# Attention and experts in one pipelined kernel: another order of the small steps in the second half of each batch

## The chip, the cores and the metric

The kernel runs on one core of a Trainium2 chip. The metric is the device time of one execution in microseconds (us). All engines of the core take part: TensorE (PE in the rows, its weight loads PEld), VectorE (DVE), ScalarE (ACT), GpSimd (POOL), and SyncE (SP), which issues most of the transfers.

## What is computed

One transformer layer in float32 on an input of 32 batches with 256 tokens of 128 values. Cut to what matters:

```
x = x + attn(layernorm(x))
x = x + ffn(layernorm(x))

attn: q, k, v of 16 heads with 8 values each
      s = q @ k.T * scale                       # 256 x 256 for each head
      s = s - max(s, axis=-1)
      w = stablemax3(s) / sum(stablemax3(s))    # s <= 0: 1 / (1 - s * (1 - 0.5 * s * (1 - s / 3)))
      out = (w @ v) @ w_out.T + b_out

ffn:  probs = softmax(x @ router_w + router_b)  # 4 experts, the best 2 are kept
      gates = the two best, scaled to a sum of 1, zero elsewhere
      h = silu(x @ w1[e]) * (x @ w3[e])         # 512 values for each expert
      out = sum over e of gates[e] * (h @ w2[e])
```

## The kernel before, in words

The batches go through a pipeline written by hand. For every step `n` each engine's program has a `first_half` and a `second_half`, and works in them on several batches at once: batch `n-2` is in its experts, batch `n-1` in the output projection, the second normalization and the router, batch `n` in the attention weights, batch `n+1` in its scores, and batch `n+2` in its first normalization and its queries and keys. Steps -2 to 3 and the last four are written out; between them a loop runs over two steps in a pass. There is no scheduler: the order of the calls in each engine's program is the order in which the engine works, and semaphores (`wait_ge`, and `after`, which waits when the count is above zero) tie the engines together.

In the first half TensorE makes the distances of eight pairs of heads (`distance(u)`, line 1263, q_stack and k_pad) and between them the two products of each of eight pairs of expert blocks (`up_a_unit` and `up_b_unit`, line 1175). ScalarE squares each distance (line 611, w_sq) and applies silu to each first product (line 620). VectorE makes the polynomial (line 810, poly) and the product of silu and second product (line 802, hid), and GpSimd multiplies hid by the gates (`gate_hidden`, line 454). One PSUM bank holds every first product (`up_a`) and most second products share `up_b`, so that product u waits until silu and hid of the one before have read the banks.

In the second half TensorE makes the scores in four portions (`score(g)`, line 1400) and between them the experts' output (`down(c, e)`, line 1417) into `up_b`. Around these stand the small steps that the change moves: `router_operand` (line 1432) transposes the second normalization xn2, `queries_operand` (line 1440) the first normalization xn, `maxima_T` (line 1456) the split row maxima, `router_logits` (line 1448) makes the logits, and `weighted_values` (line 1193) the attention's sums, one call for each of four groups of heads. The transposes all go to one PSUM bank, `misc`. The logits go to columns of `up_b` behind those of the experts' sum.

VectorE meanwhile reduces the scores to maxima (line 887, eight times), copies the router's operand out (`router_T`, line 866), splits the maxima (lines 937 and 939), adds the bias to the logits (line 919), copies the transposed maxima out (`maxima_out`, line 947), and adds the experts' sum (`experts_added`, line 912, with semaphore `acc_ok`). The first product of the next experts that is written to `up_b` waits for that sum and for the logits:

```
if u == 0:
    after(pe, acc_ok, m)
    pe.wait_ge(lg_ok, m + 1)
up(u, b_bank[u], w3_hi, w3_lo, b_full)
```

ScalarE spends the second half on logarithm and exponential of the attention weights (lines 690 and 695, four times each), with the start value of the reciprocal root (lines 705 and 708) after the first and the exponential of the router's logits (line 726) ahead of the last. A table load stands ahead of each half (lines 603 and 681). GpSimd takes the variance with eps (line 493) and half of it (line 495), then the last gating `gate_hidden(7)`, the Newton step (lines 501 to 512), and the normalized values xn2 and xn (line 517).

Of the kernel before, what the change touches and what calls it, by code (L numbers as in the profile page):

```python
# [5 lines left out]
def attention_then_experts_kernel(nc: bass.Bass, x: bass.AP, w_qkv: bass.AP, w_out: bass.AP, b_out: bass.AP,  # L6
# [52 lines left out]
    with ctx:  # L59
# [374 lines left out]
        def _(pool):  # L434
# [50 lines left out]
            def second_half(i, off):  # L485

                lo, hi = (0 if has(i, off - 1) else C), (2 * C if has(i, off + 2) else C)
                if lo < hi:
                    n = no(i, off)
                    k = n + 2  # L490
                    s = slice(lo, hi)
                    pool.wait_ge(agg_ok, k + 1)
                    nc.gpsimd.tensor_tensor(var_eps[:, s], mean_var[:, s, 1], eps_all[:, s], ALU.add).then_inc(var_ok, 1)
                    pool.wait_ge(var_ok, k + 1)
                    nc.gpsimd.tensor_tensor(half_var[:, s], var_eps[:, s], minus_half[:, s],
                                            ALU.mult).then_inc(newton_step, 1)
                if has(i, off - 2):
                    gate_hidden(no(i, off) - 2, UP - 1)
                if lo < hi:
                    pool.wait_ge(rstd0_ok, k + 1)  # L500
# [98 lines left out]
        def _(act):  # L599
# [78 lines left out]
            def second_half(i, off):  # L678
# [22 lines left out]
                if lo < hi:  # L701
                    k = n + 2
                    s = slice(lo, hi)
                    act.wait_ge(var_ok, k + 1)
                    nc.scalar.activation(ln_var[:, s], var_eps[:, s], ACT.Ln).then_inc(lnv_ok, 1)
                    act.wait_ge(lnv_ok, k + 1)
                    after(act, rstd_ok, k)
                    nc.scalar.activation(rstd0[:, s], ln_var[:, s], ACT.Exp, scale=-0.5).then_inc(rstd0_ok, 1)
# [10 lines left out]
                for g in range(G):  # L719
                    if has(i, off) and g < G - 1:  # L720
                        log_of(g + 1)
                    if g == G - 1 and has(i, off - 1):
                        m = n - 1
                        act.wait_ge(shift_ok, m + 1)
                        after(act, gates_ok, GATE * m)
                        nc.scalar.activation(exp_l[:], shifted[:], ACT.Exp).then_inc(exp_ok, 1)
                    if has(i, off):
                        weights_of(g)
                if isinstance(i, int) and n == 0:
                    act.wait_ge(ld_w3, 16)  # L730
                    high_weights(1, w3_hi)
# [35 lines left out]

            act.wait_ge(consts_v, 1)
            over_batches(act, first_half, second_half)
            drain()  # L770


        @block.vector
        def _(dve):
# [82 lines left out]
            def second_half(i, off):  # L857
                n = no(i, off)
                def router_T():
                    m = n - 1  # L860
                    dve.wait_ge(xn2T_full, m + 1)
                    if has(i, off + 2):
                        dve.wait_ge(xnT_full, n + 3)
                    after(dve, xn2_lo_ok, m)
                    after(dve, lg_full, m)
                    nc.vector.tensor_copy(xn2_T[:], misc[:, 0:S]).then_inc(xn2_out, 1)
# [129 lines left out]
                if has(i, off + 1):  # L996
                    split_maxima()
                if has(i, off - 1):
                    biased_logits()
                    shifted_logits()  # L1000
                if has(i, off + 1):
                    maxima_out()
                if has(i, off - 2):
                    experts_added()
                if has(i, off + 2) and not (isinstance(i, int) and n == -1):
# [152 lines left out]
        def _(pe):  # L1158
# [219 lines left out]
            def second_half(i, off):  # L1378
# [56 lines left out]
                def queries_operand():  # L1435
                    m = n + 2
                    pe.wait_ge(xn_ok, m + 1)
                    after(pe, v_ok, m)
                    for c in range(C):
                        last = nc.tensor.transpose(misc[:, S + c * 128:S + (c + 1) * 128], xn[:, c, :], ident[:])  # L1440
                    last.then_inc(xnT_full, 1)

                def router_logits():
                    m = n - 1
                    pe.wait_ge(xn2_out, m + 1)
                    for c in range(C):
                        cs = slice(c * 128, (c + 1) * 128)
                        last = nc.tensor.matmul(router_out[:, c, :], xn2_T[:, cs], rw[:], start=True, stop=True)
# [37 lines left out]
                if filling:  # L1486
                    spare_products(up_b, 4)
                down(1, 1)
                down(1, 2)
                score(3)  # L1490
                if has(i, off - 1):
                    router_operand()
                if has(i, off + 2):
                    queries_operand()
# [9 lines left out]
                if has(i, off):  # L1504
                    weighted_values(i, off, 0)
                if has(i, off - 1):
                    router_logits()
                if has(i, off) and not (isinstance(i, int) and n == 0):
                    weighted_values(i, off, 1)
                if has(i, off + 1) and not (isinstance(i, int) and n == 0):  # L1510
                    maxima_T()
                if isinstance(i, int) and n == -1:
# [110 lines left out]
```

## Time and profile before

| what | value |
|---|---|
| median of 3 runs | 1161.71 us (1161.48 to 1162.41) |
| time of the profiled execution | 1162.64 us |
| span in its trace | 1160.7 us |
| granted TensorE clock, mean | 0.998 |
| busy: PE, PEld | 1119.9 us (96%), 964.6 us (83%) |
| busy: DVE, ACT, POOL | 974.2 us (84%), 1006.7 us (87%), 709.3 us (61%) |

The span runs from the first to the last instruction, and 1.9 us of the profiled execution's time lie outside it. A step of the pipeline is some 34.3 us long. A TensorE row's duration covers the latency of its matmuls, which overlap each other, so that short waits hide inside the busy time; they are read from the distance between the starts of two rows.

### The profile page before, as it was taken

Reading aid. Unit: us, or ns where it says so; the run is one execution under the profiler, and the core shown is the slowest. Engines: PE = TensorE matmul, PEld = TensorE weight load, DVE = VectorE, ACT = ScalarE, POOL = GpSimd, SP = SyncE. Lnnn points to the kernel's source line nnn. Section 1 sums busy time; section 2 is a strip of 40 time slices with the busy share of each in tenths; the row PEclk is TensorE's granted clock in tenths of the full one; section 3 lists DMA queues with packets and bytes.
Section 4 is the critical chain, followed back from the end, with each engine's and each line's share of the span. In section 5 each row is a group of like instructions: output and inputs, shape, how many; then the busy total and the mean of one; then the engine's idle time right before and its main releaser. Section 6 shows DMA issues by size and latency. Waiting matters only on the chain.

```text
span 1160.7 us, 30031 instructions
## 1 busy us (share of the span) xinstructions
PE 1119.9 (96%) x10360; PEld 964.6 (83%) x10360; DVE 974.2 (84%) x1821; ACT 1006.7 (87%) x1034; POOL 709.3 (61%) x941
## 2 busy tenths in 40 slices
PE   6889999999999999999999999999999999999998
PEld 5768888788888888888888888888888888888888
DVE  4878888898888889888889888898988888988844
ACT  0799899998889998889998888999888999888882
POOL 5346665767665667666576766566766657676530
PEclk9999999999999999999999999999999999999999
DMA  4543332233332233333223343223333322333100
GB/s 119 173 138 115 116 106 85 80 117 119 123 104 89 88 99 118 119 114 97 86 82 117 119 123 104 87 87 102 118 119 112 98 85 85 119 120 120 30 6 10
DMA packets 129204, 117.54 MB, mean 101 GB/s; under 512 B 15560, under 2 KB 123784, under 8 KB 129160
## 3 DMA queue, kind: packets, MB, share of 16 engines
q1 hardware_dynamic: 126952, 113.81, 32.0%
q10 hardware_dynamic: 2208, 3.15, 0.8%
q8 instruction: 27, 0.44, 0.2%
q14 instruction: 17, 0.14, 0.0%
HBM read 94.70 MB, written 21.09 MB: 100 GB/s over the span
## 4 chain that ended last, share of the span: by engine, by line
POOL 30%; PE 28%; issue 21%; DMA 11%; DVE 4%; ACT 3%; POOLq 1%; SPq 1%; ACTq 0%; DVEq 0%
POOL hid L454 19%; PE banks L1417 11%; DMA gate_all<-gate_scratch 9%; PE banks L1175 5%; POOL qk_split L473 3%; PE sc L1400 2%; PE sc L1263 2%; PE banks L1193 2%; POOL qk_split L470 2%; POOL xn_lo L533 1%; ACT poly L690 1%; POOL xn_hi L530 1%; DVE mx L887 1%; POOL x_resb L560 1%; PE misc L1432 1%
## 5 line engine op out<-in xcount | busy, mean ns | idle before, releaser
L454 POOL TENSOR_TENSOR hid<-hid,gate_all 128x512 f32<-128x512 f32 x240 | 380.5, 1623 | 179.1 <-DMA gate_all<-gate_scratch 144.5
L810 DVE SCALAR_TENSOR_TENSOR poly<-w_sq,sc 128x1024 f32<-128x1024 f32 x252 | 303.8, 1216 | 53.0 <-ACT w_sq L611 49.4
L611 ACT ACTIVATE w_sq<-sc 128x1024 f32<-128x1024 f32 x252 | 255.4, 1027 | 92.4 <-PE sc L1263 86.6
L1175 PE MATMUL banks<-xn_hi,w_hi 128*128 128x256 f32 x976 | 288.5, 296 | 6.3 <-issue 6.3
L1175 PE MATMUL banks<-xn_hi,w_lo 128*128 128x256 f32 x976 | 275.1, 282 | 0.0
L1175 PE MATMUL banks<-xn_lo,w_hi 128*128 128x256 f32 x976 | 274.6, 281 | 0.0
L690 ACT ACTIVATE poly<-poly,two 128x2048 f32<-128x2048 f32 x128 | 254.9, 1991 | 0.4
L1417 PE MATMUL banks<-w_sb,hid 128*128 128x128 f32 x1920 | 242.9, 280 | 7.8 <-POOL hid L454 6.5
L1417 PEld LDWEIGHTS banks<-w_sb,hid 128*128 128x128 f32 x1920 | 223.4, 192 | 24.0 <-POOL hid L454 12.6
L695 ACT ACTIVATE poly<-poly 128x2048 f32<-128x2048 f32 x128 | 242.6, 1896 | 0.0
L887 DVE TENSOR_REDUCE mx<-sc 128x4 f32<-128x1024 f32 x192 | 227.5, 1214 | 15.3 <-PE sc L1400 8.7
L1175 PEld LDWEIGHTS banks<-xn_hi,w_hi 128*128 128x128 f32 x976 | 184.1, 189 | 30.1 <-issue 24.0
L1175 PEld LDWEIGHTS banks<-xn_lo,w_hi 128*128 128x128 f32 x976 | 184.1, 189 | 0.0
L1175 PEld LDWEIGHTS banks<-xn_hi,w_lo 128*128 128x128 f32 x976 | 183.2, 188 | 0.0
L1263 PE MATMUL sc<-q_stack,k_pad 128*128 128x256 f32 x1008 | 164.2, 290 | 4.0 <-DMA q_stack<-m_split 2.8
L802 DVE TENSOR_TENSOR hid<-silu_a,banks 128x512 f32<-128x512 f32 x240 | 160.7, 680 | 1.7 <-ACT silu_a L620 1.1
L1263 PEld LDWEIGHTS sc<-q_stack,k_pad 128*128 128x128 f32 x1008 | 134.3, 189 | 18.6 <-issue 11.3
L620 ACT ACTIVATE silu_a<-banks 128x512 f32<-128x512 f32 x240 | 143.8, 599 | 0.7
L1193 PE MATMUL banks<-poly,v_pad 128*32 128x256 f32 x2048 | 137.1, 385 | 0.3 <-ACT poly L695 0.2
L1193 PEld LDWEIGHTS banks<-poly,v_pad 128*32 128x32 f32 x2048 | 53.6, 109 | 41.3 <-ACT poly L695 10.0
L887 DVE TENSOR_REDUCE mx<-banks 128x4 f32<-128x1024 f32 x64 | 77.8, 1216 | 0.0
L1400 PE MATMUL sc<-k_tile,q_tile 32*128 32x256 f32 x768 | 65.1, 329 | 7.7 <-DMA q_tile<-qk_scratch 2.8
(179 smaller groups left out, 1310.2 us busy)
## 6 DMA issues: line engine op xcount, KB each, us to landing
qk_scratch<-qk_split SPq DMA_DIRECT2D x32, 512.0 KB, 3.1
k_tile<-qk_scratch SPq DMA_DIRECT2D x128, 128.0 KB, 2.6
k_pad<-qk_scratch SPq DMA_DIRECT2D x256, 64.0 KB
q_tile<-qk_scratch SPq DMA_DIRECT2D x124, 128.0 KB, 2.6
q_stack<-qk_scratch SPq DMA_DIRECT2D x124, 128.0 KB
gate_all<-gate_scratch SPq DMA_DIRECT2D x30, 512.0 KB, 4.4
x_in<-in_L_attn_x_dram SPq DMA_DIRECT2D x32, 128.0 KB, 2.1
x_res<-in_L_attn_x_dram SPq DMA_DIRECT2D x32, 128.0 KB, 2.3
```

The costliest lines, as they stand in the source:

```text
L454: nc.gpsimd.tensor_tensor(h, h, by_token.unsqueeze(1).to_broadcast([128, 2, C, 128]), ALU.mult).then_inc(gated, 1)
L611: nc.scalar.activation(w_sq[:, u % 2, :], distance_buf(n, u), ACT.Square).then_inc(sq_ok, 1)
L620: nc.scalar.activation(silu_a[:, u % 2, :], up_a[:], ACT.Silu).then_inc(silu_ok, 1)
L690: nc.scalar.activation(poly[:, C * g:C * (g + 1), :], poly[:, C * g:C * (g + 1), :], ACT.Ln, bias=two[:]).then_inc(ln_ok, 1)
L695: nc.scalar.activation(poly[:, C * g:C * (g + 1), :], poly[:, C * g:C * (g + 1), :], ACT.Exp, scale=-1.0).then_inc(p_ok, 1)
L802: nc.vector.tensor_tensor(hid[:, 2 * u:2 * u + 2, :].rearrange("p a t -> p (a t)"), silu_a[:, u % 2, :], b_bank[u], ALU.mult).then_inc(hid ...
L810: nc.vector.scalar_tensor_tensor(poly[:, u, :], w_sq[:, u % 2, :], 3.0, distance_buf(n, u), ALU.add, ALU.mult).then_inc(poly_ok, 1)
L887: nc.vector.tensor_reduce(by_row[:, :, :, u], score_buf[u].rearrange("p (j c t) -> p j c t", j=2, c=C), AX.X, ALU.min, negate=True).then_i ...
L1175: last = nc.tensor.matmul(dst, lhs[a], rhs[b], start=(k == 0), stop=(k == len(terms) - 1))
L1193: last = nc.tensor.matmul(pv[32 * j:32 * j + 32, g // 2, :], v_pad[par][:, c, 4 * g + j, first:first + 32], poly[:, 2 * g + j // 2, at:at ...
L1263: last = nc.tensor.matmul(dst[:, at:at + S], k_pad[par][:, u, j, c * 128:(c + 1) * 128], q_stack[par][:, u, :], start=True, stop=True)
L1417: last = nc.tensor.matmul(up_b[:, c * D:(c + 1) * D], hid[:, FB * e + f, c * 128:(c + 1) * 128], w2_sb[:, FB * e + f, :], start=(e == 0 an ...
```

## The change

It puts steps in another order, and alters the waits that go with the order. No multiplication, copy or transfer is added or removed, apart from one operand of the logarithm of the variance.

```
 (GpSimd, second half)
+                    if has(i, off - 2):
+                        gate_hidden(n - 2, UP - 1)
                     pool.wait_ge(agg_ok, k + 1)
                     nc.gpsimd.tensor_tensor(var_eps[:, s], mean_var[:, s, 1], eps_all[:, s], ALU.add).then_inc(var_ok, 1)
...
-                if has(i, off - 2):
-                    gate_hidden(no(i, off) - 2, UP - 1)
 (ScalarE, second half)
-                    act.wait_ge(var_ok, k + 1)
-                    nc.scalar.activation(ln_var[:, s], var_eps[:, s], ACT.Ln).then_inc(lnv_ok, 1)
+                    act.wait_ge(agg_ok, k + 1)
+                    nc.scalar.activation(ln_var[:, s], mean_var[:, s, 1], ACT.Ln, bias=eps_all[:, 0:1]).then_inc(lnv_ok, 1)
...
                 for g in range(G):
                     if has(i, off) and g < G - 1:
                         log_of(g + 1)
-                    if g == G - 1 and has(i, off - 1):
-                        m = n - 1
-                        act.wait_ge(shift_ok, m + 1)
-                        after(act, gates_ok, GATE * m)
-                        nc.scalar.activation(exp_l[:], shifted[:], ACT.Exp).then_inc(exp_ok, 1)
                     if has(i, off):
                         weights_of(g)
+                if has(i, off - 1):
+                    m = n - 1
+                    act.wait_ge(shift_ok, m + 1)
+                    after(act, gates_ok, GATE * m)
+                    nc.scalar.activation(exp_l[:], shifted[:], ACT.Exp).then_inc(exp_ok, 1)
 (VectorE, second half)
                 def router_T():
                     dve.wait_ge(xn2T_full, m + 1)
-                    if has(i, off + 2):
-                        dve.wait_ge(xnT_full, n + 3)
...
                     split_maxima()
+                if has(i, off - 2):
+                    experts_added()
+                if has(i, off + 1):
+                    maxima_out()
                 if has(i, off - 1):
                     biased_logits()
                     shifted_logits()
-                if has(i, off + 1):
-                    maxima_out()
-                if has(i, off - 2):
-                    experts_added()
 (TensorE, second half)
                 def queries_operand():
                     after(pe, v_ok, m)
+                    if has(i, off - 1):
+                        pe.wait_ge(xn2_out, n)
...
                 def router_logits():
                     pe.wait_ge(xn2_out, m + 1)
+                    after(pe, acc_ok, m)
...
                 down(1, 1)
+                if has(i, off - 1):
+                    router_operand()
                 down(1, 2)
                 score(3)
-                if has(i, off - 1):
-                    router_operand()
-                if has(i, off + 2):
+                if isinstance(i, int) and n <= 0:
                     queries_operand()
                 down(1, 3)
...
                     weighted_values(i, off, 0)
+                if has(i, off) and not (isinstance(i, int) and n == 0):
+                    weighted_values(i, off, 1)
+                if has(i, off + 2) and not (isinstance(i, int) and n <= 0):
+                    queries_operand()
+                if has(i, off + 1) and not (isinstance(i, int) and n == 0):
+                    maxima_T()
                 if has(i, off - 1):
                     router_logits()
-                if has(i, off) and not (isinstance(i, int) and n == 0):
-                    weighted_values(i, off, 1)
-                if has(i, off + 1) and not (isinstance(i, int) and n == 0):
-                    maxima_T()
```

The headings in brackets name the engine and are not part of the diff. ScalarE's program waits once more at its very start, for the constants of GpSimd (`consts_ok`).

On TensorE, late in the second half of step 3, this is the order before (names lose their numbers here: misc<-ident,xn is the transpose of xn2 at line 1432 and of xn at line 1440, and one matmul here is two in the trace):

```order
L1417 MATMUL banks<-w_sb,hid 128x128 x8
L1400 MATMUL sc<-k_tile,q_tile 128x256 x8
L1432 MATMUL misc<-ident,xn 128x128 x2
L1440 MATMUL misc<-ident,xn 128x128 x2
L1417 MATMUL banks<-w_sb,hid 128x128 x4
L1193 MATMUL banks<-poly,v_pad 32x256 x8
L1448 MATMUL banks<-rw,xn_T 128x4 x2
L1193 MATMUL banks<-poly,v_pad 32x256 x8
L1456 MATMUL misc<-ident,mx_split 32x128 x2
```

And this is the order there in the changed kernel, where line 1430 is the router's operand and line 1440 still the queries':

```order
L1415 MATMUL banks<-w_sb,hid 128x128 x4
L1430 MATMUL misc<-ident,xn 128x128 x2
L1415 MATMUL banks<-w_sb,hid 128x128 x4
L1398 MATMUL sc<-k_tile,q_tile 128x256 x8
L1415 MATMUL banks<-w_sb,hid 128x128 x4
L1191 MATMUL banks<-poly,v_pad 32x256 x16
L1440 MATMUL misc<-ident,xn 128x128 x2
L1457 MATMUL misc<-ident,mx_split 32x128 x2
L1449 MATMUL banks<-rw,xn_T 128x4 x2
```

The router's operand has moved ahead of four products and the last scores, the queries' operand behind two groups of weighted values, and the logits behind both of these and the maxima.

On VectorE, behind the last maxima of a step, this is the order before (xn_T at line 907 is the queries' operand on its way out):

```order
L937 TENSOR_SCALAR mx_split<-mx 128x4x8
L939 SCALAR_TENSOR_TENSOR mx_split<-mx,mx_split 128x4x8
L919 TENSOR_TENSOR logits<-banks,router_b_all 128x4 x2
L926 TENSOR_REDUCE top_l<-logits 128x2
L929 TENSOR_TENSOR shifted<-logits,top_l 128x8
L947 COPY m_split<-misc 32x256
L912 TENSOR_TENSOR y_acc<-banks,y_acc 128x256
L907 COPY xn_T<-misc 128x256
```

And this is it after:

```order
L935 TENSOR_SCALAR mx_split<-mx 128x4x8
L937 SCALAR_TENSOR_TENSOR mx_split<-mx,mx_split 128x4x8
L910 TENSOR_TENSOR y_acc<-banks,y_acc 128x256
L945 COPY m_split<-misc 32x256
L917 TENSOR_TENSOR logits<-banks,router_b_all 128x4 x2
L924 TENSOR_REDUCE top_l<-logits 128x2
L927 TENSOR_TENSOR shifted<-logits,top_l 128x8
L905 COPY xn_T<-misc 128x256
```

The experts' sum comes first now, and the logits come behind the copy of the maxima.

On GpSimd, at the change from first to second half, this is the order before:

```order
L454 TENSOR_TENSOR hid<-hid,gate_all 128x512 x7
L493 TENSOR_TENSOR var_eps<-mean_var,eps_all 128x4
L495 TENSOR_TENSOR half_var<-var_eps,minus_half 128x4
L454 TENSOR_TENSOR hid<-hid,gate_all 128x512
L501 TENSOR_TENSOR newton<-rstd 128x4
```

And this is it after:

```order
L454 TENSOR_TENSOR hid<-hid,gate_all 128x512 x8
L495 TENSOR_TENSOR var_eps<-mean_var,eps_all 128x4
L497 TENSOR_TENSOR half_var<-var_eps,minus_half 128x4
L500 TENSOR_TENSOR newton<-rstd 128x4
```

The eighth gating has moved ahead of the two small steps of the variance.

## Rows read from the trace of the kernel before

**Rows 1.** The profile's page: busy times, and the chain that ended last by line
```profile
PE 1119.9 (96%) x10360; PEld 964.6 (83%) x10360; DVE 974.2 (84%) x1821; ACT 1006.7 (87%) x1034; POOL 709.3 (61%) x941
...
POOL hid L454 19%; PE banks L1417 11%; DMA gate_all<-gate_scratch 9%; PE banks L1175 5%; POOL qk_split L473 3%; PE sc L1400 2%; PE sc L1263 2%; PE banks L1193 2%; POOL qk_split L470 2%; POOL xn_lo L533 1%; ACT poly L690 1%; POOL xn_hi L530 1%; DVE mx L887 1%; POOL x_resb L560 1%; PE misc L1432 1%
```

**Rows 2.** Line 1432: count, duration, first and last start
```profile
L1432 PE MATMUL misc<-ident,xn x62: 272/273/330, 83.4 to 1111.7; 128*128 128x128 f32 x62
```

**Rows 3.** Timeline, TensorE, second half: start, duration, engine, line, [idle before <- releaser]
```profile
593.88 2.05 PE L1417 MATMUL banks<-w_sb,hid 128*128 128x128 f32 x16 [0.17 <-POOL hid L454]
...
598.72 0.44 PE L1432 MATMUL misc<-ident,xn 128*128 128x128 f32 x2
...
600.20 1.07 PE L1193 MATMUL banks<-poly,v_pad 128*32 128x256 f32 x16
...
601.74 1.07 PE L1193 MATMUL banks<-poly,v_pad 128*32 128x256 f32 x16
602.74 0.39 PE L1456 MATMUL misc<-ident,mx_split 128*32 128x128 f32 x2
...
603.57 0.28 PE L1175 MATMUL banks<-xn_hi,w_lo 128*128 128x256 f32 x1
604.11 0.36 PE L1175 MATMUL banks<-xn_hi,w_hi 128*128 128x256 f32 x1 [0.27 <-issue]
604.30 0.28 PE L1175 MATMUL banks<-xn_lo,w_hi 128*128 128x256 f32 x1
```

**Rows 4.** Timeline, ScalarE, the start of two first halves in a row
```profile
572.60 0.60 ACT L620 ACTIVATE silu_a<-banks 128x512 f32<-128x512 f32 x1
...
606.89 0.60 ACT L620 ACTIVATE silu_a<-banks 128x512 f32<-128x512 f32 x1
...
610.47 0.60 ACT L620 ACTIVATE silu_a<-banks 128x512 f32<-128x512 f32 x1
```

**Rows 5.** Timeline, VectorE, hid of the second pair, the same two halves
```profile
576.82 0.69 DVE L802 TENSOR_TENSOR hid<-silu_a,banks 128x512 f32<-128x512 f32 x1
...
611.19 0.69 DVE L802 TENSOR_TENSOR hid<-silu_a,banks 128x512 f32<-128x512 f32 x1
```

**Rows 6.** Timeline, TensorE, the third pair of the experts' products
```profile
611.46 0.28 PE L1175 MATMUL banks<-xn_hi,w_hi 128*128 128x256 f32 x1
...
612.29 0.28 PE L1175 MATMUL banks<-xn_lo,w_hi 128*128 128x256 f32 x1
```

**Rows 7.** Timeline, ScalarE and VectorE, an early first half
```profile
91.82 0.60 ACT L620 ACTIVATE silu_a<-banks 128x512 f32<-128x512 f32 x1
...
94.85 0.66 ACT L620 ACTIVATE silu_a<-banks 128x512 f32<-128x512 f32 x1
...
95.64 0.68 DVE L802 TENSOR_TENSOR hid<-silu_a,banks 128x512 f32<-128x512 f32 x1
```

**Rows 8.** Timeline, VectorE, second half
```profile
599.41 0.42 DVE L866 COPY xn_T<-misc 128x256 f32<-128x256 f32 x1 [0.65 <-PE misc L1440]
...
602.13 0.18 DVE L937 TENSOR_SCALAR mx_split<-mx 128x32 fp32r<-128x32 f32 x1
...
602.46 0.22 DVE L919 TENSOR_TENSOR logits<-banks,router_b_all 128x4 f32<-128x4 f32 x2
...
603.61 0.40 DVE L912 TENSOR_TENSOR y_acc<-banks,y_acc 128x256 f32<-128x256 f32 x1
```

**Rows 9.** Timeline, GpSimd, from first to second half, and one step later
```profile
591.86 0.19 POOL L493 TENSOR_TENSOR var_eps<-mean_var,eps_all 128x4 f32<-128x4 f32 x1
...
592.28 1.54 POOL L454 TENSOR_TENSOR hid<-hid,gate_all 128x512 f32<-128x512 f32 x1
...
595.01 1.57 POOL L517 TENSOR_SCALAR xn<-y_acc,mean_var,rstd 128x128 f32<-128x128 f32 x2 [0.19 <-issue]
...
624.71 1.54 POOL L454 TENSOR_TENSOR hid<-hid,gate_all 128x512 f32<-128x512 f32 x1 [0.96 <-DVE hid L802]
```

**Rows 10.** All waits of the span: us in total, times, longest
```profile
PEld sc L1263 <- DMA q_stack<-m_split: 4.9, 12, 0.4
```

More of the change, by code:

```diff
@@ L496, in second_half @@
                                             ALU.mult).then_inc(newton_step, 1)
-                if has(i, off - 2):
-                    gate_hidden(no(i, off) - 2, UP - 1)
-                if lo < hi:
                     pool.wait_ge(rstd0_ok, k + 1)
@@ L768, in _ @@
             act.wait_ge(consts_v, 1)
+            act.wait_ge(consts_ok, 3)
             over_batches(act, first_half, second_half)
```

## The prediction

> **What bounds the kernel now.** I read the page first. TensorE is busy for 96% of the span, VectorE and ScalarE for 84% and 87%, and the chain that ended last spends most on GpSimd's gating (19%) and the transfer of the gates (9%) [rows 1]. Neither settles it: rows of matmuls overlap, so a busy TensorE may still wait, and the gating chain has room, as a rival below shows. So I took one step of the pipeline from the timeline and looked for waits that end last.
>
> The router's operand appears as 62 matmuls, two for each of 31 steps, the first at 83.4 us and the last at 1111.7. That is 1028.3 / 30 = 34.3 us a step [rows 2]. Of these 30 steps I count 28 as steady, all but the first and the last.
>
> In the second half TensorE waits in two places. The fourth portion of the experts' output starts 0.17 us late, for the last gating on GpSimd [rows 3]. And the first product into the shared bank up_b starts at 604.11, 0.54 us behind the matmul before it at 603.57, where neighbours stand 0.12 apart (seven distances make 612.29 - 611.46 = 0.83): 0.42 us lost [rows 3, 6]. The profile names no releaser there, but the code waits for the experts' sum, which VectorE does from 603.61 for 0.40 us, to 604.01 [rows 8]. These are the 0.59 us a step on which the change works.
>
> What is behind that? In the first half ScalarE goes from the first silu to the second in 610.47 - 606.89 = 3.58 us [rows 4]. In the early half at 91.82 the same five operations take 94.85 - 91.82 = 3.03 us [rows 7]. So ScalarE has little to spare there now (0.55 us), and is the next to bind.
>
> **The change, part by part.**
>
> *Gating ahead of the variance.* The last gating starts at 591.86 in place of 592.28, where the variance stood, or up to 0.1 later [rows 9]. It ends 0.3 to 0.4 us earlier, and the wait of 0.17 is gone. Gain on TensorE 0.17 (no more, since it arrives then). In exchange the two small steps, 591.86 to 592.28 with their distance, now stand behind the gating: xn2, now from 595.01 to 596.58, comes later by 0.42 less what the gating moved up, 0 to 0.25 us. ScalarE takes the variance itself and keeps its time.
>
> *Router's operand earlier.* It stood at 598.72 [rows 3]. It now comes ahead of eight matmuls and the last scores. At 0.12 each the eight take about 1.0, the scores about 0.45 us (an estimate from the distance of their neighbours), so with the 0.17 it stands near 597.1. xn2 is there between 596.6 and 596.85: no wait, by 0.25 us at the least. Queued behind it, if it did wait, are the last scores, and behind these the last two maxima of VectorE. VectorE loses a wait of 0.65 us ahead of its copy of this operand [rows 8], since it no longer waits for the queries' transposes, so the split of the maxima moves from 602.13 to about 601.45.
>
> *Experts' sum first.* It follows the split directly, where the bias stood. By the rows there it starts about 0.35 us behind 601.45, at 601.8, and ends at 602.2 instead of 604.01. The 0.42 us of TensorE is gone. The wait is now asked of the logits, which come later than they did. Weighted values start at 600.20, less 0.17, less 0.22 for the queries' operand that has left its place, at 599.8. Two groups of 1.00 (602.74 - 601.74) bring 601.8, two transposes for the queries 602.0, two for the maxima 602.15. The sum is there at 602.2: a tie, and I take a wait of 0 to 0.1.
>
> *Weighted values in twos.* Before, two groups and the logits between them take 602.74 - 600.20 = 2.54 us, which leaves 2.54 - 2.00 = 0.54 for the logits [rows 3]. After, the logits' four matmuls at 0.12 stand among their like, 0.45 to 0.48. I take 0.06 to 0.09 for that, and 0 to 0.1 for the two groups that now touch, which the trace does not show in the steady steps. So 0.06 at least, 0.19 at most.
>
> The Trainium skill, "TensorEngine Tiling (Array Packing)", Key Properties, says that a change of the tiling mode drains TensorE. By that rule the pair alone would save nothing here: weighted values and maxima use 32 columns, all else in this stretch 128, and the queries' operand, put between them, brings back the two changes that the logits leave. The gain of this part by the rule would be 0, and TensorE's whole saving 0.59. No run here shows a drain by itself.
>
> *Bias and logits behind the maxima's copy.* The copy of the maxima needs the transposes of 602.0 to 602.15, the bias then follows the logits. The first product into up_b needs them 0.7 us after the logits' last matmul, behind six other products. That work hides them; without it some 0.3 us would be open. The exponential of the logits moves behind the last weights on ScalarE. Its work is the same, its reader on VectorE stands behind the copy of queries and keys, and I cost it at nothing; if it were late, the gates' store would be, and the gating has 0.96 us of room [rows 9].
>
> TensorE thus can arrive earlier by 0.17 + 0.42 = 0.59 at least, and with the middle of the rest about 0.7 us.
>
> **What the step can use.** ScalarE's chain from the last silu of a step through two table loads and eight long passes has no gap and is not changed. From the first silu on it can shrink as in the early half. What TensorE waits for there is hid of the second pair. It starts 611.19 - 606.89 = 4.30 us behind the first silu in one step and 576.82 - 572.60 = 4.22 in the other [rows 4, 5], and 95.64 - 91.82 = 3.82 in the early half [rows 7]. That gives 0.48 and 0.40, on average 0.44. Then the second matmul of the third pair's second product: it stands at 612.29, 1.10 behind that hid [rows 5, 6]. If TensorE stands waiting, it is 0.69 for hid, 0.19 from the first matmul after a wait to the second (604.30 - 604.11, where 0.12 is usual) [rows 3, 5], and a latency that I don't know, 0.88 at least. So 0 to 0.22 more; I take 0.10, nearer the middle since some latency is certain. Sum: 0.44 + 0.10 = 0.54 us a step, less than the 0.59 to 0.78 that TensorE can give. Past this place the first half stays as it is, shifted as a whole.
>
> 28 steps x 0.54 = 15.1 us. The first steps and the drain I leave at 0. From the profiled execution's 1162.64 us (its span 1160.7 and 1.9 outside) that makes 1147.5. The median of the runs is 0.9 below that execution, so 1146.6.
>
> **Rivals.**
>
> *New waits take part of it.* The operand of the router, the split of the maxima and the experts' sum all arrive within 0.25 us of being asked for, and a wait brings its refill of 0.07. The spare is 0.05 to 0.24. Waits of 0.2 to 0.5 in sum leave 0.1 to 0.4 a step: 1150.5 to 1159.4, about 1154. The mode rule above speaks for this case. For it also: the store of the maxima, for which the weight loads of the distances now wait up to 0.4 us, 12 times [rows 10]; against it, the maxima's copy moves up as much as TensorE.
>
> *ScalarE does not hold it.* Then TensorE's 0.78 counts in full: 28 x 0.78 = 21.8, 1139.9. Against it stands the early half, whose 3.03 us hold no gap.
>
> *The gating chain is the bound*, as the page's chain has it: transfer, eight gatings, output. Then only ends would move, 1161.7 give or take 2. Against it: GpSimd idles for 0.96 us ahead of the seventh gating, waiting for hid [rows 9], so the loop through the transfer has that much room.
>
> *Slower.* xn2 comes too late, the router's operand waits, and the last scores and two maxima wait behind it. The price is what xn2 lacks beyond 0.25 us. It decides from 0.25 + 0.7, some 0.95 us of further lateness, on: only then is TensorE later than before. At 1.15 us it would cost 28 x 0.2 = 5.6, 1167. For it: GpSimd's steps depend on each other one by one. Against: each of the rows is 0.2 us.
>
> **How the numbers follow.** Chances: forecast 0.60 (its own range 1142.5 to 1150.5: 0.40 to 0.70 us a step), part of it 0.20, TensorE in full 0.07, gating chain 0.07, slower 0.06. Measurements of this kernel tell 0.2%, 2.3 us, from no change. Faster holds the first three, 0.87; within 0.2% the fourth, 0.07; slower 0.06. The range 1141 to 1156 holds the forecast, three quarters of the second case and some of the third.
>
> **What would show it.** The idle times of 0.17, 0.27 and 0.65 us [rows 3, 8] are gone. From first to second silu 3.0 to 3.1 us, and a new wait of TensorE for hid or silu at the third pair. The distance of the router's operands falls to 33.7. The prediction is wrong if that distance of silus stays at 3.5, if TensorE waits at the router's operand or at the logits for more than 0.2 us, or if ScalarE shows a gap between its passes.

## The result, and the profile after

The changed kernel takes **1150.03 us** (median of five runs, 1149.25 to 1151.11) where the kernel before took 1162.41 beside it (1161.48 to 1162.72): a ratio of 0.9897 (95% interval 0.9882 to 0.9911). It is faster by 12.4 us. The forecast was 1146.6 in a range of 1141 to 1156: right in direction and inside the range, with a gain of 15.1 us promised. It lies at the slow end of the forecast's own range, 1142.5 to 1150.5.

The page of the changed kernel, against [rows 1]:

```profile
PE 1120.0 (98%) x10360; PEld 969.3 (84%) x10360; DVE 981.3 (85%) x1821; ACT 1002.0 (87%) x1034; POOL 708.8 (62%) x941
...
PE 89%; ACT 4%; DVE 3%; issue 1%; DMA 1%; ACTq 0%; SPq 0%; DVEq 0%
```

TensorE's busy time is what it was, in a shorter span (1148.1 us). The chain that ended last runs now 89% over TensorE, instead of over the gating and its transfer. Taken by itself this says that TensorE is the bound; the experiments show that it isn't.

The router's operand (line 1430 now), against [rows 2], and the logarithm of the variance, each with count, duration and first and last start:

```profile
L1430 PE MATMUL misc<-ident,xn x62: 272/273/330, 81.9 to 1098.1; 128*128 128x128 f32 x62
L704 ACT ACTIVATE ln_var<-mean_var,eps_all x34: 279/282/298, 4.0 to 1093.5; 128x4 f32<-128x4 f32 x29, 128x2 f32<-128x2 f32 x5
```

A step takes 1016.2 / 30 = 33.87 us where it took 34.28: 0.41 us less, not 0.54. Over thirty steps that is 12.1 us. The first operand stands 1.5 us earlier, and what follows the last is 1.0 us longer (1148.1 - 1098.1 = 50.0, before 49.0). The sum is the 12.6 us between the spans. The second row is to be kept in mind: 282 ns.

TensorE in a second half and the next first half, against [rows 3] and [rows 6]:

```profile
589.15 1.16 PE L1415 MATMUL banks<-w_sb,hid 128*128 128x128 f32 x8
590.14 0.38 PE L1430 MATMUL misc<-ident,xn 128*128 128x128 f32 x2
...
592.87 1.93 PE L1191 MATMUL banks<-poly,v_pad 128*32 128x256 f32 x32
594.74 0.44 PE L1440 MATMUL misc<-ident,xn 128*128 128x128 f32 x2
595.01 0.38 PE L1457 MATMUL misc<-ident,mx_split 128*32 128x128 f32 x2
595.23 0.52 PE L1449 MATMUL banks<-rw,xn_T 128*128 128x4 f32 x4
595.61 0.37 PE L1173 MATMUL banks<-xn_hi,w_hi 128*128 128x256 f32 x1
...
596.28 0.28 PE L1173 MATMUL banks<-xn_hi,w_lo 128*128 128x256 f32 x1
596.40 0.28 PE L1173 MATMUL banks<-xn_hi,w_hi 128*128 128x256 f32 x1
...
603.20 0.63 PE L1261 MATMUL sc<-q_stack,k_pad 128*128 128x256 f32 x4
603.80 0.39 PE L1173 MATMUL banks<-xn_hi,w_hi 128*128 128x256 f32 x1
604.03 0.28 PE L1173 MATMUL banks<-xn_lo,w_hi 128*128 128x256 f32 x1
...
604.51 0.28 PE L1173 MATMUL banks<-xn_hi,w_lo 128*128 128x256 f32 x1
604.71 0.39 PE L1173 MATMUL banks<-xn_hi,w_hi 128*128 128x256 f32 x1
604.93 0.28 PE L1173 MATMUL banks<-xn_lo,w_hi 128*128 128x256 f32 x1
```

And of the kernel before, what has to be set beside it:

```profile
593.43 0.28 PE L1400 MATMUL sc<-k_tile,q_tile 32*128 32x256 f32 x2
...
596.29 2.05 PE L1417 MATMUL banks<-w_sb,hid 128*128 128x128 f32 x16
...
602.89 0.36 PE L1175 MATMUL banks<-xn_hi,w_hi 128*128 128x256 f32 x1
...
610.99 0.64 PE L1263 MATMUL sc<-q_stack,k_pad 128*128 128x256 f32 x4
```

The place of the lost 0.42 us is closed: the first product into up_b starts at 596.40, 0.12 behind 596.28 like any other. New is what stands at the third pair. Its first product starts 0.60 us behind the distances (before 611.46 - 610.99 = 0.47), and the matmul after it 0.23 behind it instead of 0.12. The second product, which waits for hid, shows the same (0.20 and 0.22, before 0.12 and 0.12). These four distances are longer than before by 0.13 + 0.11 + 0.08 + 0.10 = 0.42 us: so much TensorE now stands waiting there. The two groups of weighted values take 594.74 - 592.87 = 1.87 us, less than the 2 x 1.00 of [rows 3], and the logits 0.38 instead of 0.54. But the maxima's transposes take 0.22 instead of 0.15, and the last portion of the experts' output, which now follows the scores directly, 1.09 instead of 0.99. In all, from the start of `down(1, 1)` to the first product of the next experts, it is 595.61 - 589.15 = 6.46 us, before 602.89 - 596.29 = 6.60.

ScalarE over the same stretch, against [rows 4]:

```profile
594.96 3.70 ACT L694 ACTIVATE poly<-poly 128x2048 f32<-128x2048 f32 x2
598.56 0.19 ACT L727 ACTIVATE exp_l<-shifted 128x8 f32<-128x8 f32 x1
598.77 1.28 ACT L602 ACT_TABLE_LOAD   x1
600.06 0.60 ACT L619 ACTIVATE silu_a<-banks 128x512 f32<-128x512 f32 x1
...
603.10 0.66 ACT L619 ACTIVATE silu_a<-banks 128x512 f32<-128x512 f32 x1
```

ScalarE goes from its last weights through the logits' exponential and the table load to silu without a gap, and from silu to silu in 603.10 - 600.06 = 3.04 us instead of 3.58.

VectorE, against [rows 8] and [rows 5]:

```profile
591.52 0.41 DVE L864 COPY xn_T<-misc 128x256 f32<-128x256 f32 x1
...
594.28 0.18 DVE L935 TENSOR_SCALAR mx_split<-mx 128x32 fp32r<-128x32 f32 x1
...
594.61 0.42 DVE L910 TENSOR_TENSOR y_acc<-banks,y_acc 128x256 f32<-128x256 f32 x1
...
603.97 0.68 DVE L802 TENSOR_TENSOR hid<-silu_a,banks 128x512 f32<-128x512 f32 x1
```

The wait of 0.65 us ahead of the operand's copy is gone. The experts' sum ends at 595.03, 0.20 us before the logits, so TensorE doesn't wait for it. Hid of the second pair comes 603.97 - 600.06 = 3.91 us behind the first silu: before 4.30 and 4.22, in the early half of [rows 7] 3.82. In the changed kernel's steps from 159 us on it is 3.91 to 3.94, and in the last four 3.81 or 3.82.

### The profile page after: what moved, and what is told of

It is laid out like the page before. It is cut to its first block, busy times and chain, and to the rows that moved or that the text cites. A ratio compares the mean times of both kernels' runs of the same rounds, so it can differ in the third digit from the quotient of the medians.

```text
span 1148.1 us, 30045 instructions
## 1 busy us (share of the span) xinstructions
PE 1120.0 (98%) x10360; PEld 969.3 (84%) x10360; DVE 981.3 (85%) x1821; ACT 1002.0 (87%) x1034; POOL 708.8 (62%) x941
## 4 chain that ended last, share of the span: by engine, by line
PE 89%; ACT 4%; DVE 3%; issue 1%; DMA 1%; ACTq 0%; SPq 0%; DVEq 0%
PE banks L1173 32%; PE banks L1415 20%; PE sc L1261 10%; PE banks L1191 10%; PE sc L1398 3%; ACT poly L689 2%; ACT poly L694 1%; PE misc L1467 1%; PE misc L1307 1%; PE misc L1468 1%; PE misc L1325 1%; PE banks L1398 1%; PE misc L1286 1%; DVE mx L885 1%; PE misc L1316 1%
## 5 line engine op out<-in xcount | busy, mean ns | idle before, releaser
L1173 PE MATMUL banks<-xn_hi,w_hi 128*128 128x256 f32 x976 | 291.9, 299 | 0.1
L1415 PE MATMUL banks<-w_sb,hid 128*128 128x128 f32 x1920 | 250.5, 281 | 1.5 <-DVE hid L802 0.6
L694 ACT ACTIVATE poly<-poly 128x2048 f32<-128x2048 f32 x128 | 239.6, 1895 | 0.0
L1191 PE MATMUL banks<-poly,v_pad 128*32 128x256 f32 x2048 | 130.7, 384 | 1.0 <-DVE mx L885 0.7
L1191 PEld LDWEIGHTS banks<-poly,v_pad 128*32 128x32 f32 x2048 | 56.7, 109 | 46.9 <-issue 10.5
L537 POOL TENSOR_TENSOR equal<-equal,earlier 128x16 f32<-128x16 f32 x62 | 12.4, 221 | 113.6 <-DVE equal L952 113.6
```

The lines of the kernel that those rows point to most:

```text
L694: nc.scalar.activation(poly[:, C * g:C * (g + 1), :], poly[:, C * g:C * (g + 1), :], ACT.Exp, scale=-1.0).then_inc(p_ok, 1)
L1173: last = nc.tensor.matmul(dst, lhs[a], rhs[b], start=(k == 0), stop=(k == len(terms) - 1))
L1191: last = nc.tensor.matmul(pv[32 * j:32 * j + 32, g // 2, :], v_pad[par][:, c, 4 * g + j, first:first + 32], poly[:, 2 * g + j // 2, at:at ...
L1415: last = nc.tensor.matmul(up_b[:, c * D:(c + 1) * D], hid[:, FB * e + f, c * 128:(c + 1) * 128], w2_sb[:, FB * e + f, :], start=(e == 0 an ...
```

## The experiments

The theory: TensorE arrives early enough, and what holds the step is ScalarE's chain up to the first silu, then silu and hid of the second pair, and behind these TensorE's own work in the rest of the first half. Of the 0.54 us 0.09 is lost to the operand that the logarithm got, the rest to hid. The rivals: TensorE's own stride (98% busy) holds the step, or new waits in the second half do. The step is read in every kernel as above, from the first and last router's operand.

| kernel | median us | kernel before, same chip | ratio [95%] | step us |
|---|---|---|---|---|
| before | | | | 34.28 |
| after | 1150.03 | 1162.41 | 0.9897 [0.9882, 0.9911] | 33.87 |
| a_nobias | 1147.08 | 1161.81 | 0.9873 [0.9857, 0.989] | 33.79 |
| a_pe2 | 1151.77 | 1161.81 | 0.9914 [0.9898, 0.9931] | 33.93 |
| a_pe6 | 1178.72 | 1161.81 | 1.0146 [1.0129, 1.0163] | 34.79 |
| a_act | 1155.77 | 1161.81 | 0.995 [0.9933, 0.9966] | 34.06 |
| p_gate | 1155.31 | 1162.1 | 0.9942 [0.9924, 0.996] | 34.03 |
| u_gate | 1150.85 | 1162.1 | 0.99 [0.9883, 0.9918] | 33.90 |
| u_operand | 1159.61 | 1162.1 | 0.9976 [0.9966, 0.9985] | 34.18 |
| p_tail | 1167.15 | 1162.1 | 1.0044 [1.0029, 1.0059] | 34.45 |
| b_bias (one run) | 1162.41 | 1161.7 | | 34.28 |
| n_expbias | 1159.03 | 1161.7 | 0.998 [0.9971, 0.9989] | 34.14 |
| best_vT | 1138.14 | 1161.7 | 0.9803 [0.979, 0.9817] | 33.49 |
| b_vT | 1161.36 | 1161.7 | 0.9999 [0.999, 1.0008] | 34.25 |

**a_nobias: after, without the logarithm's operand.** The start value is taken from the variance without eps; the Newton step keeps eps.

```diff
-nc.scalar.activation(ln_var[:, s], mean_var[:, s, 1], ACT.Ln, bias=eps_all[:, 0:1]).then_inc(lnv_ok, 1)
+nc.scalar.activation(ln_var[:, s], mean_var[:, s, 1], ACT.Ln).then_inc(lnv_ok, 1)
```

> The changed kernel, but the logarithm of the variance takes mean_var without the eps tile as bias. The start value of the root is then taken from the variance without eps; the Newton step still uses the variance with eps. Theory (ScalarE's chain holds the step; the bias operand made this logarithm 0.09 us longer, 0.282 for 0.188 us): its duration falls to 0.19 us, the step from 33.91 to 33.82 us, and the time by 28 x 0.09 = 2.5 us, to 1147.5. Rival 1 (the stride of mean_var is what makes it longer): duration stays 0.28, no change. Rival 2 (TensorE, 98% busy and 89% of the chain, holds the step): duration falls, but the time stays at 1150.

```profile
L704 ACT ACTIVATE ln_var<-mean_var x34: 186/189/207, 3.9 to 1091.0; 128x4 f32<-128x4 f32 x29, 128x2 f32<-128x2 f32 x5
```

The instruction falls from 282 to 189 ns, 0.093 us, and the step from 33.87 to 33.79. The whole run is 2.95 us shorter than after (each beside its own runs of the kernel before: 0.0024 of 1162, 2.8 us). Nothing was taken from TensorE. So a tenth of a microsecond on ScalarE counts nearly in full, and the rival of TensorE's stride falls.

**a_pe2 and a_pe6: after, with needless float32 products on TensorE** ahead of the first of the experts' products in every step.

```diff
                 if u == 0:
                     pe.wait_ge(xn2_lo_ok, m + 1)
+                    spare_products(up_a, 2)      # a_pe6: 6
```

> The changed kernel with two needless matmuls of 128 columns, 0.12 us each, in every step, on TensorE ahead of the first product of the experts. Theory (in the first half TensorE waits for silu and hid of the second pair, with 0.3 to 0.4 us to spare): 0 to 0.05 us a step, under 1.5 us in all; the first silus keep their distance of 3.03 us. Rival (TensorE holds the step): 0.24 us a step, 30 steps, 7 us, to 1157.

> The same with six needless matmuls, 0.71 us a step. Theory: the spare of 0.3 to 0.4 us is used up and the rest, 0.3 to 0.4 us, counts: 9 to 12 us, to about 1160. Rival (TensorE holds the step): 0.71 us x 30 = 21 us, to 1171.

The row of a_pe2's products:

```profile
596.66 0.69 PE L1167 MATMUL banks<-ident 128*128 128x128 f32 x4
```

I had sized the load wrong. Each call stands as two matmuls of 0.11 us, so that two calls add 0.45 us and six 1.34, not 0.24 and 0.71. What they cost is 0.06 and 0.92 a step. The spare of TensorE ahead of the third pair is thus 1.34 - 0.92 = 0.42 from the one and 0.39 from the other, which is what the four distances above add up to. In the trace of a_pe2 these are back at 0.47 and 0.12. That six calls came out at 1178.72 and not near 1160 is this load; had TensorE held the step, they would have cost 30 x 1.34 = 40 us, and they cost 28.7. TensorE is busy 98% of the time and yet 0.4 us early in every step.

**a_act: after, with one needless exponential on ScalarE** ahead of the table load.

```diff
+                    nc.scalar.activation(extra[:], ident[:], ACT.Exp)
```

> The changed kernel with one needless exponential of 128x128 on ScalarE behind that of the router's logits, ahead of the table load, in every step. It is 0.2 to 0.3 us long by its neighbours. Theory (ScalarE's chain holds the step): all that it adds between the last weights and the first silu counts, 28 x 0.2 to 0.3 = 6 to 8 us, to 1156 to 1158. Rival (TensorE holds the step): ScalarE's addition is hidden, 1150.

```profile
600.34 0.20 ACT L728 ACTIVATE exp_l<-shifted 128x8 f32<-128x8 f32 x1
600.44 0.29 ACT L729 ACTIVATE extra<-ident 128x128 f32<-128x128 f32 x1
600.74 1.28 ACT L603 ACT_TABLE_LOAD   x1
```

Between the starts of the logits' exponential and the table load there are now 0.40 us, where after had 0.21: 0.19 more. The step is 0.19 longer. What ScalarE gets counts one for one, what TensorE gets (0.45 us) hardly counts.

**b_bias: before, with a zero tile as the logarithm's bias.** It separates the operand's price from the change.

```diff
-nc.scalar.activation(ln_var[:, s], var_eps[:, s], ACT.Ln).then_inc(lnv_ok, 1)
+nc.scalar.activation(ln_var[:, s], var_eps[:, s], ACT.Ln, bias=zero[:]).then_inc(lnv_ok, 1)
```

> The kernel before, in which the logarithm of the variance keeps its operand var_eps, without gaps in memory, but takes a tile of zeros as bias. If the bias tile is what cost the 0.09 us, its duration is 0.28 us in place of 0.19; if it was the stride of mean_var, 0.19.

```profile
L705 ACT ACTIVATE ln_var<-var_eps,zero x34: 278/283/298, 4.2 to 1105.9; 128x4 f32<-128x4 f32 x29, 128x2 f32<-128x2 f32 x5
```

The row of before is 188 ns; the tile alone, holding zeros, makes 283 of it. The step stays at 34.28: before, ScalarE had the time to spare.

**n_expbias: a_nobias, with the zero tile on the four long exponentials of a step.**

```diff
-                                         scale=-1.0).then_inc(p_ok, 1)
+                                         bias=zero[:], scale=-1.0).then_inc(p_ok, 1)
```

> The kernel without the eps bias, in which the four long exponentials of every step take a tile of zeros as bias as well. If a bias tile costs about 0.095 us whatever the size (1.99 us with, 1.90 without, for the logarithm and the exponential of 128x2048), their duration rises to 1.99. Theory (ScalarE's chain holds the step): 4 x 0.095 x 28 = 10.6 us more, 1147 to 1158. Rival (TensorE holds it): no change.

The group of these exponentials (busy in all, mean ns of one), in n_expbias, and then in a_nobias:

```profile
L694 ACT ACTIVATE poly<-poly,zero 128x2048 f32<-128x2048 f32 x128 | 251.5, 1989 | 0.0
```

```profile
L694 ACT ACTIVATE poly<-poly 128x2048 f32<-128x2048 f32 x128 | 239.6, 1895 | 0.0
```

Again 94 ns each, on an instruction ten times as long: the price doesn't grow with the size. Four make 0.376 us, and the step grows by 0.35, the run by 12 us. That is nearly all of what the change under study brought, lost to one argument.

**p_gate: before, with only the gating ahead of the variance** (and the logarithm with its bias).

```diff
+                    if has(i, off - 2):
+                        gate_hidden(n - 2, UP - 1)
                     pool.wait_ge(agg_ok, k + 1)
...
-                if has(i, off - 2):
-                    gate_hidden(no(i, off) - 2, UP - 1)
```

> The kernel before with only the last gating ahead of the variance, and with it the logarithm from mean_var with the eps tile as bias. Theory (before, TensorE's waits in the second half held the step, and ScalarE had 0.55 us to spare): the wait of 0.17 us goes, 28 x 0.17 = 5 us, to about 1157, and the logarithm's 0.09 us are hidden there. Rival (the longer logarithm counts in any case): 28 x 0.08 = 2 us, to about 1160.

**u_gate: after, with the gating behind the variance again** (the same lines the other way round).

> The changed kernel with the last gating back behind the variance. Theory (TensorE has 0.42 us to spare a step in the changed kernel): the wait of 0.17 us comes back in the second half and is hidden, 0 to 1 us, 1150. Rival (each part of the change gives its own share): 5 us, 1155.

TensorE of p_gate, and then of u_gate, at the place of the wait:

```profile
589.88 0.28 PE L1400 MATMUL sc<-k_tile,q_tile 32*128 32x256 f32 x2
590.09 2.05 PE L1417 MATMUL banks<-w_sb,hid 128*128 128x128 f32 x16
```

```profile
588.01 2.05 PE L1415 MATMUL banks<-w_sb,hid 128*128 128x128 f32 x16 [0.20 <-POOL hid L454]
```

Alone in the kernel before the gating brings 0.25 us a step, 0.6% of the run, more than the 0.17 that was expected of it. The wait of 0.17 had a price behind it too: from the scores to the experts' output it was 593.88 - 593.43 = 0.45 us before and is 590.09 - 589.88 = 0.21 in p_gate, 0.24 less. So the logarithm's longer operand took nothing from the gain here, as in b_bias. Taken out of the changed kernel it costs 0.03 a step, though TensorE's wait of 0.20 us is back for all to see: it goes into the 0.4 us by which TensorE is early. The parts' shares don't add up.

**p_tail: before, with only the new order behind the last scores** (and the logits' exponential behind the last weights): both groups of weighted values ahead of the maxima, the logits behind them, and the experts' sum directly behind the split. The router's operand stays where it was.

```diff
                 split_maxima()
+                experts_added()
+                maxima_out()
...
-                    router_logits()
...
+                    router_logits()      # behind maxima_T
```

> The kernel before with only the tail in the new order: two groups of weighted values in a row, the experts' sum first, maxima, logits behind; gating, variance and both operands as before. Theory: the 0.42 us for the experts' sum are given back as a wait of TensorE for the split of the maxima, which VectorE has no earlier than before: 0 to 2 us gained, 1160 to 1162. Rival (the sum's wait alone was the loss): 28 x 0.42 = 12 us, 1150.

```profile
570.25 0.40 PE L1457 MATMUL misc<-ident,mx_split 128*32 128x128 f32 x2 [0.52 <-DVE mx_split L939]
570.68 0.58 PE L1449 MATMUL banks<-rw,xn_T 128*128 128x4 f32 x4
```

A miss: I had looked for a small gain, and it loses 0.17 us a step. With the logits no longer between them, TensorE comes to the maxima before VectorE has split them, waits 0.52 us, and the logits stand in the queue behind. In the mean of some 20 steps the stretch from `down(1, 1)` to the next experts' first product grows from 6.59 to 7.19 us; the 0.42 for the experts' sum come off that, which leaves the 0.17.

**u_operand: after, with both transposed operands behind the last scores again.**

```diff
-                if has(i, off - 1):
-                    router_operand()
                 down(1, 2)
                 score(3)
+                if has(i, off - 1):
+                    router_operand()
+                if has(i, off + 2):
+                    queries_operand()
```

> The changed kernel with both operands' transposes (router's and queries') back behind the last scores. Theory: VectorE waits 0.65 us again ahead of the router's copy, the split of the maxima comes that much later, and TensorE, with two groups of weighted values in a row, waits for it; the first product into the shared bank comes 0.5 to 0.6 us later than in the changed kernel, 0.1 to 0.2 us more than the spare: 3 to 5 us, to 1153 to 1155. Rival (the operand's place does not matter, since the transposes only change places): 1150.

TensorE, and then VectorE, of this kernel:

```profile
600.43 0.40 PE L1457 MATMUL misc<-ident,mx_split 128*32 128x128 f32 x2 [0.47 <-DVE mx_split L939]
600.86 0.58 PE L1449 MATMUL banks<-rw,xn_T 128*128 128x4 f32 x4
```

```profile
597.25 0.42 DVE L866 COPY xn_T<-misc 128x256 f32<-128x256 f32 x1 [0.65 <-PE misc L1440]
...
599.97 0.18 DVE L937 TENSOR_SCALAR mx_split<-mx 128x32 fp32r<-128x32 f32 x1
```

The direction was expected, the size not: 0.31 us a step, most of the gain (expected were 1153 to 1155 us). VectorE waits its 0.65 us again for the queries' transposes, the split comes late by as much, and TensorE waits 0.47 at the maxima, as in p_tail. The same stretch takes 7.19 us against 6.46 of the changed kernel, 0.73 more and not the 0.5 to 0.6 expected; less the spare of 0.42 that makes the 0.31. So the early operand is what makes the new order behind it pay. A kernel with the sum early and the logits in their old place was not tried, so what the logits' place alone is worth stays open.

**best_vT: a_nobias, with the transposes of the attention's sums (`values_T`, o_T at line 1307) put where TensorE waits.** They stood behind the third pair's products.

```diff
                 distance(2)
-                ups(2)
                 values_T()
+                ups(2)
```

> The kernel without the eps bias, and in the first half TensorE transposes the attention's sums (line 1307, four matmuls, 0.45 us) ahead of the third pair of the experts' products instead of behind it. Theory: TensorE waits there for silu and hid of the second pair, 0.4 to 0.5 us with the refills; the transposes fill the wait, and the distances behind them come that much earlier: 28 x 0.3 to 0.45 = 8 to 12 us, 1147 to 1135 to 1139. Rival (TensorE, 98% busy, holds the step): no change, 1147.

**b_vT: before, with the same move alone.**

> The kernel before with only that move of the transposes. Theory: before the change TensorE arrived at the third pair 0.35 us after silu, so there is no wait to fill: 0 us, 1162. Rival (the move helps by itself, whatever else is changed): 8 to 12 us.

TensorE of best_vT:

```profile
596.84 0.64 PE L1261 MATMUL sc<-q_stack,k_pad 128*128 128x256 f32 x4
597.32 0.60 PE L1307 MATMUL misc<-ident,o_T 128*128 128x128 f32 x4
597.67 0.36 PE L1173 MATMUL banks<-xn_hi,w_hi 128*128 128x256 f32 x1
597.87 0.28 PE L1173 MATMUL banks<-xn_lo,w_hi 128*128 128x256 f32 x1
```

best_vT takes 1138.14 us (1137.68 to 1139.48), 8 to 9 us less than a_nobias (0.9803 of the kernel before, against 0.9873) and 2% less than before. The four transposes, 0.35 us long, stand where TensorE would have waited, and are gone from the place behind, where they held the step; it is 0.30 us shorter. In the kernel before, where TensorE came later and had no such wait, the same move brings nothing. Together the two show that the wait at the third pair is real, and new.

## Why the prediction was right, and what it had wrong

**TensorE's part held.** The waits of 0.17 and 0.42 us are gone, the operand finds xn2 ready, and the sum is there before the logits. The "tie" was sized too cautiously, since there is a spare of 0.20. The prediction moved VectorE's split up by 0.68 us, for its wait of 0.65. From the first maxima to the split it is 602.13 - 591.64 = 10.49 us before and 594.28 - 584.73 = 9.55 after, 0.94 less: a second wait of VectorE, 0.18 us for scores that stood behind the late gating, is gone too. The row is of the kernel before:

```profile
596.40 1.23 DVE L887 TENSOR_REDUCE mx<-sc 128x4 f32<-128x1024 f32 x1 [0.18 <-PE banks L1400]
```

The prediction had TensorE 0.59 to 0.78 us earlier, and more than it could use. What it couldn't use would have been 0.7 - 0.54 = 0.16; measured are 0.4. Part of it is that the step uses less (0.41), part that TensorE gave some 0.8 rather than 0.7. Its three parts are 0.24 for the gating (0.17 in the prediction, which left out what a wait costs behind it, though its own rival has that as "refill"), 0.42 for the sum, and 6.60 - 6.46 = 0.14 for the new order, for which the prediction had 0.06 to 0.19.

**The bound that takes over was named rightly.** Silu to silu 3.04 us (forecast 3.0 to 3.1), the new wait at the third pair, no gap on ScalarE. a_act, a_pe2 and a_pe6 show it: ScalarE's time counts in full, that of TensorE ahead of the third pair only beyond 0.4 us.

**Two terms were mis-sized.** The first stands in the sentence that ScalarE's chain "has no gap and is not changed". It was changed: the logarithm got a tile as its bias, 282 ns instead of 188. This is 0.09 us a step of the 0.13 missing, shown by a_nobias (0.08 in the step, 2.95 us in the run). The diff had it in plain sight; I costed it as the same instruction. The Trainium skill, "ScalarE: Activation LUTs", What ACT_TABLE_LOAD costs, gives some 93 ns for each pointer operand of an ACTIVATE beyond what immediate operands take. The three pairs of rows here agree with it (189 and 282, 188 and 283, 1895 and 1989 ns), and the prediction should have had it.

The second is the 0.44 us for hid. It was taken from the early half, where hid came 3.82 us behind silu. In the steady step it comes after 3.91, so this part gives 0.39 and 0.31, on average 0.35. The other term, the third pair's second product, gives 0.14 rather than 0.10: from hid to that product's second matmul are 604.93 - 603.97 = 0.96 us instead of 1.10 [rows 5, 6]. Together 0.49 less 0.09 make 0.40, and 0.41 was measured. So the errors partly offset each other, and the result lies at the lower end of the forecast's 0.40 to 0.70 us a step, where the rival of new waits (0.1 to 0.4) begins; it is the rows and not the time that tell the two apart. Why hid needs 0.09 more than in the early half was not tried. The traces show where it arises: the first square starts 0.50 us behind silu in both (600.56 and 92.32), but VectorE's first polynomial 1.65 us behind it in the steady step (601.71) and 1.55 in the early half (93.37).

**The rivals.** New waits of TensorE in the second half: none, but p_tail and u_operand show that this rival was close. It comes true as soon as the router's operand stands behind the last scores, at 0.47 to 0.52 us and at the split of the maxima, one of the three places that the rival names. The case "slower" put the danger at xn2, which had 0.48 us to spare (ready at 589.66, asked for at 590.14):

```profile
588.09 1.57 POOL L516 TENSOR_SCALAR xn<-y_acc,mean_var,rstd 128x128 f32<-128x128 f32 x2 [0.19 <-issue]
```

ScalarE doesn't hold it: out, by a_act. The gating chain is the bound: out, since a step shrank by 0.41. The Trainium skill, "TensorEngine Tiling (Array Packing)", Key Properties, says that a change of the tiling mode drains TensorE. The prediction took from it that the weighted values in twos would save nothing. By the rows above TensorE came 0.14 us earlier by the new order with as many changes of mode. No run took this part alone, and none shows a drain by itself, so the rule is neither shown nor refuted.

**The ends** were left at 0; they gave 1.5 and took 1.0. The prediction counted 28 steps, and the 0.41 is the mean of all 30.

## What to carry to other kernels

When a wait is removed from one engine, price every instruction of the engine that binds next, down to the kind of each operand; "not changed" has to be read from the diff and not from the order. Busy shares and the chain by engine don't tell what binds: add a known bit of work to one engine at a time, and see which of it comes back in the time. And when a bound has moved, look for work that can be put into the new wait: it was worth 8 to 9 us here, and nothing before the bound moved.

## What the runs showed of the hardware

- A tile as bias, of eps or of zeros, costs an ACTIVATE 0.093 to 0.095 us at both sizes measured: 188 to 283 ns at 128x4, 1895 to 1989 ns at 128x2048.
- The first matmul that was waited for stands 0.19 to 0.23 us ahead of the next, where 0.12 is usual. A wait costs its own time and some 0.1 us more: taking away one of 0.17 us brought 0.24. The distance alone doesn't prove a wait, since the first product behind a group of weighted values has it in both kernels (601.67 to 601.89 in the changed one).
- A float32 product of 128 columns is two matmuls of 0.11 us in the trace, while a transpose of the same size is one (two in the 0.22 us from 590.14).
- Two groups of weighted values (32 columns of the array) that touch take 1.87 us, two that stand apart 2 x 1.00.
